# Cross-attention layer on one core: softmax probabilities turned by a DMA transpose instead of by TensorE

## The reference, cut to what matters

```python
def attention(q, k, v, mask):                       # 16 heads of 32 columns, 128 queries, 128 keys
    scores = einsum('bhqd,bhkd->bhqk', q, k) / sqrt(32)
    scores = scores * mask - 10000.0 * (1.0 - mask)
    probs = softmax(scores, axis=-1)
    return einsum('bhqk,bhkd->bhqd', probs, v)

# x (32, 128, 512), encoder_states (32, 128, 512), float32
q, k, v = split(layernorm(x) @ w_qkv + b_qkv)       # self attention
x = x + merge(attention(q, k, v, ltor_mask)) @ w_ao + b_ao
q = layernorm(x) @ w_q + b_q                        # cross attention
k, v = split(encoder_states @ w_kv + b_kv)
x = x + merge(attention(q, k, v, cross_mask)) @ w_co + b_co
return x + gelu(layernorm(x) @ w1 + b1) @ w2 + b2   # MLP, 512 -> 2048 -> 512
```

## Time and profile before

| | |
|---|---|
| median of 3 runs | 2080.74 us (2080.07 to 2082.67) |
| span of the profiled execution | 2081.6 us (the page gives no other time for that execution) |
| PE (matmul) busy | 1957.9 us, 94% |
| DVE busy | 1390.2 us, 67% of the whole span |
| ACT busy | 1072.6 us, 52% |
| POOL busy | 884.1 us, 42% |

### The profile page before, as it was taken

One profiled execution on the slowest core, in us unless ns is written; L12 is line 12 of the kernel. 1 busy time (PEld: TensorE's weight loads), 2 busy tenths in 40 slices (PEclk: granted clock), 3 DMA queues, 4 the chain that ended last, 5 costly groups with the idle time before them and its releaser, 6 DMA issues. The chain is left out here.

```text
span 2081.6 us, 39412 instructions
## 1 busy us (share of the span) xinstructions
PE 1957.9 (94%) x12304; PEld 1657.1 (80%) x12304; DVE 1390.2 (67%) x2571; ACT 1072.6 (52%) x2562; POOL 884.1 (42%) x910
## 2 busy tenths in 40 slices
PE   5999999999998999999999999699999999999999
PEld 5788888888787778887887887588888888888887
DVE  6889889888888998899889888662322323232221
ACT  4666666667667666666676666443222222222222
POOL 5556556556557655555565555450201012020110
PEclk9999999999999999999999999899999999999999
DMA  6332222222223432332232224501010101101010
GB/s 172 94 91 70 65 77 68 66 72 74 61 73 88 106 97 73 86 93 72 77 96 71 73 83 104 165 28 51 11 55 5 60 12 48 50 10 54 6 41 21
DMA packets 144820, 141.51 MB, mean 68 GB/s; under 512 B 20736, under 2 KB 94464, under 8 KB 144768
## 3 DMA queue, kind: packets, MB, share of 16 engines
q1 hardware_dynamic: 144768, 140.85, 24.2%
HBM read 82.07 MB, written 25.17 MB: 52 GB/s over the span
## 5 line engine op out<-in xcount | busy, mean ns | idle before, releaser
L1046 POOL TENSOR_TENSOR a_t_s<-a_t_s,a_m_add 128x512 f32<-128x512 f32 x256 | 345.4, 1349 | 334.3 <-DVE a_t_s L837 334.1
L1315 DVE TENSOR_TENSOR m_g_r<-m_g_t,m_g_r 128x512 fp32r<-128x512 f32 x128 | 95.9, 750 | 476.1 <-ACT m_g_r L1294 476.0
L1223 PE MATMUL m_ps_h<-k_bd,wt 128*128 128x512 f32 x1536 | 378.7, 397 | 2.9 <-PEq L360 2.9
L1223 PEld LDWEIGHTS m_ps_h<-k_bd,wt 128*128 128x128 f32 x1536 | 289.2, 189 | 72.4 <-issue 3.3
L1237 PE MATMUL m_ps_y<-m_down_hi,m_g_r 128*128 128x512 f32 x1024 | 343.8, 396 | 0.1
L704 ACT ACTIVATE a_p_s<-a_t_s,a_nb 128x128 f32<-128x128 f32 x1024 | 328.3, 391 | 8.3
L524 PE MATMUL a_ps_c<-a_xT,wt 128*128 128x256 f32 x2304 | 318.2, 288 | 11.6 <-DVE a_xT L885 5.5
L524 PEld LDWEIGHTS a_ps_c<-a_xT,wt 128*128 128x128 f32 x2304 | 285.4, 191 | 25.3 <-issue 10.9
L1237 PEld LDWEIGHTS m_ps_y<-m_down_hi,m_g_r 128*128 128x128 f32 x1024 | 192.4, 188 | 45.1 <-issue 0.5
L1278 ACT ACTIVATE m_g_t<-m_ps_h,bias_cols 128x512 f32<-128x512 f32 x128 | 88.1, 688 | 270.9 <-PE m_ps_h L1223 270.7
L688 ACT CAST a_pT<-a_ps_t 128x512 f16<-128x512 f32 x256 | 150.0, 586 | 150.7 <-PE a_ps_t L502 150.4
(11 more groups left out here) (85 smaller groups left out, 3210.9 us busy)
## 6 DMA issues: line engine op xcount, KB each, us to landing
k_bd<-a_k_r SPq DMA_DIRECT2D x512, 64.0 KB, 2.1
a_x_t<-in_x SPq DMA_DIRECT2D x32, 256.0 KB, 2.8
a_res_t<-in_x SPq DMA_DIRECT2D x32, 256.0 KB, 2.8
x_after_self<-a_y_t SPq DMA_DIRECT2D x32, 256.0 KB, 2.0
a_x_t<-x_after_self SPq DMA_DIRECT2D x32, 256.0 KB, 2.7
a_enc_t<-in_ctx SPq DMA_DIRECT2D x32, 256.0 KB, 2.9
raw_wt<-in_w SPq DMA_DIRECT2D x32, 256.0 KB, 4.7
a_res_t<-x_after_self SPq DMA_DIRECT2D x32, 256.0 KB, 3.9
```

What stands on the lines that cost most here:

```text
L1046: nc.gpsimd.tensor_tensor(t_s[:, n % 2], t_s[:, n % 2], m_add[:, b].unsqueeze(1).to_broadcast([P, HQ, P]), ALU.add).then_inc(s["biased"], 1)
L1223: last = nc.tensor.matmul(ps_h[j % 2][:], w1[hw][:, j // KC, kc, (j % KC) * P:(j % KC + 1) * P], xT[:, hx, kc], start=(k == 0), stop=(k == ...
```

## The change

The four transposes on PE and their PSUM tiles `ps_t` go. `high_probs` and `low_probs` now read `p_s` and write a new SBUF tile `p_h` (float16, high and low halves of 512 columns each, two buffers). SP then issues one DMA transpose per slot from `p_h` (128 partitions by 1024 columns) to `pT`, `turn_probs`, after `low_probs` of that slot, first of its DMAs in the slot. `weigh_values` waits for that DMA. It stands later in PE's slot: after the chunk of queries or keys in slots 0 to 4 and 7, still ahead of outputs and chunk in slots 5 and 6. On DVE `context` moves to the end of its slot, behind the low part of the chunk. The value copies on ACT and POOL move later by up to a slot. The layer norm now works in place (`xn = x_t`), so `load_x` waits until PE has turned the row.

```diff
+        probs_in = [sem(f"probs_in{i}") for i in range(2)]
...
-            xn = buf("xn", [P, GB, H])
+            xn = x_t
...
+            p_h = buf("p_h", [P, 2, 2, HQ * P], F16)
...
-            ps_t = [ps(f"a_ps_t{i}", [P, HQ, P], F32, st) for i in range(2)]
...
                     def load_x(g, b):
                         if known(g, 1):
-                            sp.wait_ge(s["xn_done"], at(g * GB - GB + b + 1))
+                            sp.wait_ge(s["xT_done"], at(g * GB - GB + b + 1))
...
+                    def turn_probs(g, n):
+
+                        sp.wait_ge(s["ptl_done"], at(slot_no(g, n)))
+                        sp.sem_inc(s["turns_begun"], 1)
+                        sp.dma_start_transpose(
+                            pT[:, n % 2].rearrange("p h (j q) -> p (h j) q", j=HQ),
+                            p_h[:, n % 2].rearrange("p h t -> p (h t)")).then_inc(probs_in[n % 2], 16)
...
+                        if cur if n >= 2 else prev:
+                            turn_probs(*lag(g, n, 2))
...
-                    def transpose_probs(g, n):
-                        pe.wait_ge(s["exp_done"], at(slot_no(g, n)))
-
-                        if n >= 2 or known(g, 1):
-                            pe.wait_ge(s["ptl_done"], at(slot_no(*lag(g, n, 2))))
-                        for j in range(HQ):
-                            last = nc.tensor.transpose(ps_t[n % 2][:, j], p_s[:, n % 2, j], ident[:])
-                        last.then_inc(s["pt_done"], 1)
-
                     def weigh_values(g, n):
                         c, b = divmod(n, GB)
-                        pe.wait_ge(s["ptl_done"], at(slot_no(g, n)))
+                        pe.wait_ge(probs_in[n % 2], at(turned(g, n)))
...
-                        if cur if n >= 2 else prev:
-                            transpose_probs(*lag(g, n, 2))
                         if n == 5 and nxt:
                             (flip_enc if crosses(g + 1) else flip_x)(g + 1, 1)
                         if n == 6 and nxt and crosses(g + 1):
                             flip_x(g + 1, 1)
-                        if cur if n >= 3 else prev:
-                            weigh_values(*lag(g, n, 3))
...
                         if n == 7 and nxt:
                             keys(g + 1, 1)
+                        if cur if n >= 3 else prev:
+                            weigh_values(*lag(g, n, 3))
...
                     def high_probs(g, n):
-                        act.wait_ge(s["pt_done"], at(slot_no(g, n)))
+                        act.wait_ge(s["exp_done"], at(slot_no(g, n)))
...
-                        nc.scalar.copy(pT[:, n % 2, HI], ps_t[n % 2][:].rearrange("p j t -> p (j t)")
+                        nc.scalar.copy(p_h[:, n % 2, HI], p_s[:, n % 2].rearrange("p j t -> p (j t)")
...
-                            act.wait_ge(s["pt_done"], at(slot_no(*lag(g, n, 2))))
+                            act.wait_ge(s["ptl_done"], at(slot_no(*lag(g, n, 2))))
...
-                        if n in (1, 3) and cur:
-                            value_top(g, n // 2)
+                        if n == 3 and cur:
+                            value_top(g, 1)
...
-                            value_middle(g, n // 2)
+                        if n == 1 and cur:
+                            value_top(g, 0)
+                        if n in (2, 3) and cur:
+                            value_middle(g, n - 2)
...
-                        nc.vector.tensor_tensor(pT[:, n % 2, LO], ps_t[n % 2][:].rearrange("p j t -> p (j t)"),
-                                                pT[:, n % 2, HI], ALU.subtract).then_inc(s["ptl_done"], 1)
+                        nc.vector.tensor_tensor(p_h[:, n % 2, LO], p_s[:, n % 2].rearrange("p j t -> p (j t)"),
+                                                p_h[:, n % 2, HI], ALU.subtract).then_inc(s["ptl_done"], 1)
...
-                        if cur if n >= 3 else prev:
-                            context(*lag(g, n, 3), (g + 1) * GB + n if n in (1, 2) and ahead else None)
...
                         if n in (0, 1, 4, 5) and leads(g):
                             flip_x(g + n // 4, n % 4)
+                        if cur if n >= 3 else prev:
+                            context(*lag(g, n, 3))
...
-                        if n in (1, 3) and cur:
-                            value_rest(g, n // 2)
+                        if n in (2, 3) and cur:
+                            value_rest(g, n - 2)
```

More of the change, by code:

```diff
@@ L317, in lag, with turned @@
                 return (g, n - by) if n >= by else (g - 1, n - by + NS)
+            def turned(g, n):
+                return 16 * (g * (NS // 2) + n // 2 + 1)
             def slot_no(g, n):
@@ L951, in slot @@
                         if n in (1, 2) and ahead:
-                            if not prev:
-                                dve.wait_ge(s["stats_done"], (g + 1) * GB + n)
+                            dve.wait_ge(s["stats_done"], at((g + 1) * GB + n))
+                            if n == 1 and cur:
+                                low_cols(g, 2, WK, k_r, "kh_done", "kl_done")
+                            if n == 2 and cur:
+                                low_cols(g, 2, WQ, q_r, "qh_done", "ql_done")
                             moments(g + 1, n - 1)
-                        if n in (0, 2, 4) and cur:
+                        if n in ((0, 4) if ahead else (0, 2, 4)) and cur:
                             low_cols(g, n // 2 + 1, WQ, q_r, "qh_done", "ql_done")
-                        if n in (1, 3) and cur:
+                        if n in ((3,) if ahead else (1, 3)) and cur:
                             low_cols(g, (n + 3) // 2, WK, k_r, "kh_done", "kl_done")
@@ L1086, in slot @@
                         low_weights(nc.gpsimd, split_here(g, n), wt[0], True)
-                        if n in (1, 3) and cur:
-                            value_last(g, n // 2)
+                        if n in (2, 3) and cur:
+                            value_last(g, n - 2)
                         if n in (5, 7) and prev:
```

8 lines of the change are left out of this document (3 added, 5 removed).

## The result

The kernel after took 2270.3 us in the median of four runs (2238.4 to 2274.9), the kernel before on the same chip 2081.7 (2080.1 to 2085.2): a ratio of 1.085, 95% interval [1.078, 1.093]; the ratio leaves the longest of the four out as a slow run, and the two medians by themselves give 1.091. Slower was the likelier sign in the prediction, but the time lies 60 us above its range. The profiled execution (span 2273.2 us) is the longest of the four, so its waits are read by their place and size, not by their sums alone.

What follows compares the result with a forecast made beforehand. The prediction took DVE to pace slots 1 to 4 and PE the rest. It added 18 us for 30 steady groups and 5 us for the ends to 2081.6 us, giving 2104 us, range 2005 to 2210 (8 in 10).

Steps and rivals of the forecast that it cites:

- The sign: Whole kernel: slower at 0.52, faster by over 0.2% at 0.40, within that at 0.08.
- 2L + 31.7: One group of self attention: its predicted time with the lock included, 39.9 us at L = 4.1 against 39.3 before.
- L: Time from the end of low_probs to the transpose's landing: 4.1 us taken, bounds 3.1 to 4.4, break-even at 3.8.
- the rival of the short transpose: DMA transpose: bytes decide, L is 3.1 us, a group takes 37.9 us, the kernel 2044 us; chance 0.34.
- the sum over one group: Longest path from low_probs of slot 4 through one group, holding two landings: +0.6 us per group, +18 us over 30 groups.
- Both waits of slots 4 and 5 should go: PE's waits of 0.56 us for the values and 1.56 us for DVE's low part of x should vanish.
- DVE paces slots 1 to 4 with 16.2: DVE, low_probs of slot 1 to slot 4: nearly always busy, 16.0 us as before plus 0.2 for longer low_probs.
- The lock: DVE and POOL contending for SBUF's port pair: +0.5 us per group taken, bounds -1.7 to +3.
- SP, nothing for it: Issuing the transposes on SP: 4 to 20 us per group, SP under 34 us, so no cost counted.
- The ends: Last slots of attention: loads of the MLP's first rows and last transposes delayed, +5 us, bounds 0 to 15.
- the long rival: DMA transpose: L of 5.5 us, 42.7 us per group, 2188 us in all, PE's clock possibly falling; chance 0.16.
- PE paces everything: Attention: with L hidden, 3.5 us less per group, 3.1 after DVE's share, 1993 us; chance 0.06.

Runs made afterwards that it cites:

- half: Kernel after with only the high halves turned (512 columns per DMA) and used for both halves: 2221.2 us.
- pe_turn: Kernel after with the four transposes per slot back on TensorE and the casts reading PSUM, its new orders kept: 2198.8 us.
- ctx_last: Kernel before with DVE's order of after alone (context behind the chunk's low part, low parts of slots 1 and 2 ahead of the moments): 2147.9 us.
- values_late: Kernel before with one edit, the value copies on ACT and POOL up to a slot later: 2153.1 us.
- weigh_late: Kernel before with one edit, the weighing on PE placed behind the chunk of queries or keys: 2146.8 us.
- sp_both: Kernel after with the loads of x ahead of the transpose and the key pieces a slot later in SP's queue: 2269.8 us.
- no_turn_old: Kernel before with the probabilities split in SBUF and turned by no one, orders of before, layer norm in place: 2111.0 us.
- psum_no_turn_old: no_turn_old with p_s in PSUM, so that low_probs has one input outside SBUF, against the kernel before: 2079.2 us, ratio 0.998.
- fill: Kernel after with TensorE's four transposes per slot run besides, into tiles no one reads: 2239.6 us.
- values_back: Kernel after with ACT's and POOL's value copies back at the slots of the kernel before: 2282.5 us.
- ctx4: Kernel before with context moved behind the flip of x in slot 4 alone: 2065.6 us, ratio 0.991.
- idle_turn: Kernel after with every DMA transpose issued but not waited for on PE, the weighing reading unturned p_h: 2203.4 us.
- no_turn: Kernel after without any transpose, the weighing reading p_h unturned: 2196.2 us.

## Why the prediction was wrong, point by point

**The sign** was right, the size was not: +189 us against +23. The wait for the DMA, as the prediction reckoned it, was not even too cheap: 2L + 31.7 with the measured L of 3.3 gives 38.3, a *gain* of 1 us per group, where the group took 43.75 from one `low_probs` of slot 4 to the next.

**L** was mis-sized: 3.3 measured from the end of `low_probs` to the weighing, 4.1 taken. By the prediction's own words (wrong if L is under 3.8) this step failed, and by its sum it is the rival of the short transpose, priced at 2044. L lies near the bound where bytes decide, 3.1. The view of the DMA engines from 505 to 510 us, in forty slices of 0.125 us, holds one transpose and hardly anything else:

```profile
GB/s 123 29 0 0 0 0 0 0 0 0 0 0 0 0 43 215 223 207 215 215 215 199 209 184 156 17 0 0 0 0 0 0 0 0 0 0 0 0 0 0
```

The data take some 1.3 us, about as long as the prediction's bound by bytes, and the rest of the 3.1 is fixed. half agrees: half of the bytes take 0.6 us less. The page of the Trainium skill that the prediction named for 350 to 400 GB/s ("Advanced Engine Details and Errata", section "X-Bar Transpose (TRN2)") is nearer than the other, but the rate here is some 215 GB/s. The transpose of slot 0 is an exception, with 4.8 us from `low_probs` (525.43) to the weighing (530.23), because it was issued late.

**The step that failed is the sum over one group.** Its four terms, with L = 3.3 put in, against the trace (ends of `low_probs` at 505.48, 516.02, 525.43, 529.52 and 549.23):

| from `low_probs` of | predicted, us | measured, us |
|---|---|---|
| slot 4 to slot 6 | 10.3 | 10.5 |
| slot 6 to slot 0 | 7.2 | 9.4 |
| slot 0 to slot 1 | 4.1 | 4.1 |
| slot 1 to slot 4 | 16.2 | 19.7 |

The first wait for the DMA came out, and the second, in slot 7, lay hidden: PE waited for nothing there. What failed is the time of DVE's own queue in the new orders. From slot 6 to slot 0 the prediction followed PE (L, weighing, half row, scores), but the scores of slot 0 were done at 522.6 and masked only at 524.16, behind a chunk for which DVE had waited, and behind `context`:

```profile
521.76 0.86 PE L507 MATMUL a_ps_s<-k_bd,a_q_r 128*128 128x512 f32 x3
...
524.16 0.68 DVE L843 TENSOR_TENSOR a_t_s<-a_ps_s,a_m_mul 128x512 f32<-128x512 f32 x1
```

From slot 1 to slot 4 it took the 16.0 of before as they were. It took the new orders as free: DVE's early low part of x as a gain, `context` as 0.9 us in line behind the chunk, the later value copies as nothing. pe_turn gives these orders 115 us, 3.6 per group, with L out of the program. Within them the prediction put `context` where it stands and did not see what it used to cover: before, it ran while PE and ACT made the next chunk; after, DVE waits 2.46 and 1.85 us there and does it then (ctx_last: +64 us). The value copies had a room of nothing, which the earlier trace rows said: PE waited 0.56 us for them in slot 4 (values_late: +70; weigh_late: +63; together +73).

**"Both waits of slots 4 and 5 should go"**: wrong. The one for x shrank from 1.56 to 1.06, and that for the values moved, to the half row (0.68 us at 531.43). **"DVE paces slots 1 to 4 with 16.2"**: wrong; from `low_probs` of slot 1 to that of slot 4 it is now 19.7 us, of which DVE is idle for 3.6. The largest piece is 1.83 us for x (531.35), though sp_both, where x is there in time, is no faster.

**The lock**: +0.5 us per group taken. `low_probs` is 0.75 in the mean as forecast, `context`'s product fell from 0.55 to 0.48, `centre` from 1.35 to 0.74, and POOL's `add_bias` rose from 1.35 to 1.73. On DVE it is a gain in sum, but by the orders and not by the casts: in pe_turn, with the same orders and the casts from PSUM, `context`'s product is at 0.41. Where DVE paced, in the old orders, the same casts cost 32 us (no_turn_old less psum_no_turn_old). What the prediction quotes from "SBUF — State Buffer", section "SBUF: two separate sides", of the Trainium skill, that two inputs in SBUF bring a DVE operation into the contest, held for `low_probs`: with one of them in PSUM it is back at 0.68.

**SP, nothing for it**: right. An issue takes 1.25 us; late ones, and the late loads of x, are visible, and sp_both, without either, takes no less. **The ends**, +5: mis-sized as well. The nine groups outside the two steady stretches take 21 + 29 + 15 = 65 us more, where the steady 5 to 6 per group would give about 50, so some 15 belong to the ends. The last 46.7 us of attention ran at a clock of 0.71 (0.82 before). "The MLP is unchanged" was right.

**The clock** was named only beside the long rival. It is a term of its own: some 30 us, by the long and the short groups of cross attention, and fill agrees. **The DMA share** rose to 0.50 and not towards 0.8, as the prediction had said of a price of 0.041 us per run of 256 B: from the shares of 0.50 and 0.27 a run costs about 0.02, half of a 512 B packet, so bytes and not runs set the time. **The lower bound** of the range, 2005, goes by the prediction's own sum with an L of 2.45; L = 2.3 would give 1996.

**The idea itself**: the prediction asked what 3.5 us less on PE is worth and answered "where PE paces". psum_no_turn_old gives the number, under 5 us in all, in the orders of before and at the clock that PE then had. The rival "PE paces everything" (1993) had no ground, as the earlier trace rows said.

What stays open: whether the early value copies cost the kernel after anything (values_back), how the 115 us divide exactly, since +64 and +73 make 137 and overlap, how much of the +64 is `context` and how much the low parts that moved with it, and why the clock fell after three groups of cross attention and not before.

## What to carry to other kernels

Before pricing what a change removes from the busiest engine, leave it out altogether and run that: here it was worth 0.2%, far less than the rest of the change cost. Price an operation moved in a queue written out by hand by what it covers at its old place, not only by its length at the new one: look whether the instruction behind it will now wait for something that used to be ready. When a latency must be hidden by a reordering, test the reordering without it first; and if the profile shows one wait that a part of the reordering removes, do that part alone (ctx4).

## What the runs showed of the hardware

- A DMA transpose from SBUF to SBUF of 128 x 1024 float16 is issued in 1.25 us on SyncE and lands 3.1 us after the start of its issue; 128 x 512 take 1.20 and 2.5 us. While its data move the DMA engines carry some 215 GB/s. At eight per group the DMA share rises from 0.27 to 0.50. Beside other work this traffic cost 7 us in all (idle_turn against no_turn).
- The same group of cross attention took 43.8 us at a granted clock of 1.00 and 47.8 at 0.89, in one execution. More TensorE work that no one reads made that kernel 31 us faster, with the clock at 0.975 instead of 0.945 over the whole execution.
- The contest for SBUF between DVE and GpSimd lengthens all three parties at once (0.68 to 0.95, 0.55 to 0.71, 1.35 to 1.69 us), and with an operand of the new DVE operation in PSUM the first is back at 0.68 and the last at 1.35, the second at 0.63. In the kernels where DVE has slack no run gives its price by itself.
